# Moving the self-loop term of a graph layer into the adjacency chunk on the Pool, and the expert counts with it

## The chip, the cores and the metric

One core of a Trainium2 chip. Five engines work side by side and meet through semaphores: TensorE (PE), VectorE (DVE), ScalarE (ACT), GpSimd (the Pool) and SyncE (SP), which here only issues DMAs. The metric is the time of one execution in microseconds, less is better.

## The reference

```
def layer(x, adj, kernel, bias, beta, Wr, br, W1, b1, W2, b2):
    z = layernorm(x)                                  # x: 4096 x 128
    scale = 1 / (sum(adj, axis=1) + beta)
    agg = adj @ z + beta[:, None] * z                 # adj: 4096 x 4096, float32
    x = x + scale[:, None] * agg @ kernel + bias
    z = layernorm(x)
    logits = z @ Wr + br                              # 64 experts
    top2, idx = top_k(logits, 2);  gates = softmax(top2)
    return x + sum over the 2 experts e of a row: gate_e * (relu(z @ W1[e] + b1[e]) @ W2[e] + b2[e])
```

## The kernel before

The 4096 rows are cut into 32 tiles of 128. Eight groups g of four tiles (512 columns of the transposed adjacency) are worked one after the other. The adjacency of a group comes in eight chunks k of 1 MB, each holding four tiles of source rows by the group's 512 columns, by DMAs that SP issues (`load_chunk`, L373) into a ring of five buffers, `adj_sb`. A buffer is loaded again when its chunk has been read: after the DVE's `low_part` for a split chunk, after the PE's products for a whole one.

Group 0 and chunk 7 of each later group are whole: the PE multiplies float32 chunks as they are (L883). Chunks 0 to 6 of groups 1 to 7 are split: ACT rounds the chunk (`round_chunk`, L550) into one of three `high` buffers, the DVE subtracts (`low_part`, L668) into `low`, and the PE makes three products of them (L893, L894, L897). `high` of a chunk may be written when the chunk three before has been used. ACT has these chunks in one row, with the other work of the previous group between them: the copy of the sum (`copy_agg`, L554) ahead of chunk 3, the root ahead of chunk 4, `normalise` (L565) ahead of chunk 5 and `copy_z1t` (L571) ahead of chunk 6.

The term beta * z is a product of its own: the Pool copies the group's z tiles to `zi` (L474), makes `diag`, four 128 x 128 blocks identity times beta (L475), and the PE multiplies them into the same bank at the end of the group (`own_product`, L876).

The previous group is finished while the PE multiplies the present one, at fixed steps of its chunks. `gnn` (L849) stands in chunk 0, `turn_z1` (L855) at the start of chunk 4, `router` (L861) at the start of chunk 5 and `ranks` (L866 to L869) in the middle of chunk 6. The DVE does `residual`, `shifts`, and after chunk 6's `low_part` the choice of two experts (`choose`, L694 to L708), which ends with `mask`. `ranks` waits for `mask`. Then come `low_part` of the next group's chunk 0 and `place` (L712 to L719), which makes the counts `more` and `seen` and the rows' targets, `slot`.

The Pool's `dispatch(g)` copies the normalised rows to `payload` (L481, L482), waits once for `prefilled` (eight padding DMAs of the rows' DRAM tensor, which SP issues among the chunks of groups 1 and 2, L396) and for `slot`, issues eight indirect DMAs (L488, "scatters") and waits until all have landed, since all share one semaphore; `normalise(g)` waits for the landed scatters of group g - 2. `own_rows(g + 2)` stands ahead of `dispatch(g)` on the Pool.

After the eighth group a list of expert tiles is made, and the expert part runs (L950 to L966 on the PE, L507 on the Pool), then the output. The change touches none of that.

## Time and profile before

| | us |
|---|---|
| median of 3 runs | 421.05 (419.92 to 421.44) |
| the profiled execution | 419.54, of which the span of the trace is 417.7 |
| group 0 | up to 41 |
| groups 1 to 7 | 41 to 236 |
| tail of group 7 and the list | 236 to 270 |
| expert part | 270 to 393 |
| output | 393 to 418 |

Busy shares of the whole span are PE 85%, DVE 72%, POOL 56%, ACT 39%; they average stages with different limits. The group stage is read on its own: from one group's end to the next, which wait ends last, and whether it is so in every group. The time between two ends is about 27.3 us in groups 4 to 6, and 28 to 28.6 us in groups 1, 2, 3 and 7.

### The profile page before, as it was taken

What the parts mean: (1) busy time and instruction counts of PE and PEld (TensorE: products, weight loads), DVE (VectorE), ACT (ScalarE), POOL (GpSimd) and SP (SyncE); (2) the same over time, 40 slices, a digit from 0 to 9 for tenths busy, and PEclk for the clock granted to TensorE, in tenths of its full rate; (3) what the DMA queues carried; (4) which work ended last, traced back from release to release, by engine and by line L of the source; (5) the groups of instructions that cost most, each with busy time, mean ns of one, the idle gap of its engine ahead of it and who ended that gap; (6) DMA issues with size and microseconds to landing.
All of it is one profiled execution on the core that took longest, in us unless ns stands there. A gap on an engine that the chain in (4) does not pass through costs nothing.

```text
span 417.7 us, 8267 instructions
## 1 busy us (share of the span) xinstructions
PE 353.5 (85%) x2029; PEld 283.0 (68%) x2029; DVE 299.8 (72%) x881; ACT 163.7 (39%) x260; POOL 233.2 (56%) x219
## 2 busy tenths in 40 slices
PE   5999999979989999999998727199999999999300
PEld 2445777867858768778686423199999999999200
DVE  4644989779798997988987347066777777777157
ACT  3445654754845738548454030011212111112153
POOL 3450003076583885858838654246777777777600
PEclk9799999999999999999999958689999999999855
DMA  8999998997968969879691110779999999996087
GB/s 295 367 424 362 395 424 313 420 427 286 398 239 357 359 230 421 326 264 374 236 399 42 40 40 30 211 215 290 300 306 303 310 292 289 300 291 215 27 335 269
DMA packets 45479, 119.25 MB, mean 286 GB/s; under 512 B 7689, under 2 KB 19614, under 8 KB 37266
## 3 DMA queue, kind: packets, MB, share of 16 engines
q1 hardware_dynamic: 27794, 95.88, 61.9%
q10 hardware_dynamic: 12672, 14.58, 11.7%
q0 software_dynamic: 4992, 8.54, 5.7%
q8 instruction: 9, 0.15, 0.1%
q14 instruction: 12, 0.10, 0.1%
HBM read 104.02 MB, written 16.78 MB: 289 GB/s over the span
## 4 chain that ended last, share of the span: by engine, by line
PE 35%; POOL 22%; DMA 18%; issue 11%; DVE 10%; ACT 3%; POOLq 1%; SPq 0%; ACTq 0%; DVEq 0%
POOL dispatched_rows L488 16%; DMA dispatched_rows<-payload,slot 10%; PE bank L956 8%; PE bank L883 7%; PE bank L966 4%; PE bank_pair L966 4%; DMA expert_answers<-adj_ring,ans 3%; DVE adj_low L668 3%; PE bank L950 2%; POOL diag L475 2%; PE bank_pair L963 2%; PE bank L963 2%; DVE x_sb L824 2%; POOL payload L481 2%; DMA adj_ring<-adj_t 2%
## 5 line engine op out<-in xcount | busy, mean ns | idle before, releaser
L668 DVE TENSOR_TENSOR adj_low<-adj_ring,adj_high 128x2048 fp32r<-128x2048 f32 x49 | 113.8, 2332 | 27.7 <-ACT adj_high L550 27.6
L550 ACT CAST adj_high<-adj_ring 128x2048 fp32r<-128x2048 f32 x49 | 93.3, 1907 | 67.4 <-PE bank L897 40.5
L488 POOL DMA_INDIRECT dispatched_rows<-payload,slot x64 | 95.3, 1489 | 36.9 <-issue 29.0
L507 POOL DMA_INDIRECT expert_answers<-adj_ring,ans x92 | 90.5, 983 | 41.0 <-ACT adj_ring L600 20.9
L893 PE MATMUL bank<-adj_high,z_hi 128*128 128x512 f32 x196 | 79.6, 406 | 0.0
L894 PE MATMUL bank<-adj_high,z_lo 128*128 128x512 f32 x196 | 76.6, 391 | 0.0
L803 DVE TENSOR_SCALAR adj_ring<-bank,adj_ring 128x128 f32<-128x128 f32 x184 | 56.0, 346 | 14.4 <-PE bank L956 11.9
L883 PE MATMUL bank<-adj_ring,z_sb 128*128 128x512 f32 x120 | 55.9, 619 | 3.2 <-DVE z_sb L654 3.2
L956 PE MATMUL bank<-xt_sb,adj_ring 128*128 128x128 f32 x368 | 57.1, 278 | 0.0
L897 PE MATMUL bank<-adj_low,z_hi 128*128 128x512 f32 x196 | 52.7, 390 | 0.0
L956 PEld LDWEIGHTS bank<-xt_sb,adj_ring 128*128 128x128 f32 x368 | 49.5, 195 | 0.0
L474 POOL COPY zi<-z_sb 128x512 f32<-128x512 f32 x8 | 8.5, 1063 | 66.0 <-PE bank L876 37.5
L883 PEld LDWEIGHTS bank<-adj_ring,z_sb 128*128 128x128 f32 x120 | 23.7, 199 | 30.5 <-issue 29.4
L897 PEld LDWEIGHTS bank<-adj_low,z_hi 128*128 128x128 f32 x196 | 36.8, 188 | 8.1
L600 ACT COPY adj_ring<-bank_pair 128x128 f32<-128x128 f32 x46 | 11.3, 267 | 77.9 <-PE bank_pair L966 76.5
L894 PEld LDWEIGHTS bank<-adj_high,z_lo 128*128 128x128 f32 x196 | 36.9, 188 | 6.6
L893 PEld LDWEIGHTS bank<-adj_high,z_hi 128*128 128x128 f32 x196 | 36.9, 188 | 6.5
L950 PE MATMUL bank<-ident,adj_ring 128*128 128x128 f32 x92 | 26.3, 286 | 9.3 <-DMA adj_ring<-dispatched_rows 9.0
L793 DVE COPY xt_sb<-bank 128x128 f32<-128x128 f32 x92 | 25.7, 280 | 10.9 <-PE bank L950 10.9
L966 PE MATMUL bank_pair<-adj_ring 128*128 128x128 f32 x184 | 28.8, 280 | 0.4 <-DVE adj_ring L803 0.3
L966 PE MATMUL bank<-adj_ring 128*128 128x128 f32 x184 | 28.5, 277 | 0.2 <-DVE adj_ring L803 0.2
L798 DVE TENSOR_TENSOR ans<-adj_ring,skip_tab 128x1 int32<-128x1 f32 x92 | 14.7, 160 | 18.5 <-DMA expert_answers<-adj_ring,ans 15.6
(129 smaller groups left out, 430.5 us busy)
## 6 DMA issues: line engine op xcount, KB each, us to landing
adj_ring<-adj_t SPq DMA_DIRECT2D x64, 1024.0 KB, 8.9
adj_ring<-w_pack SPq DMA_DIRECT2D x48, 257.5 KB
adj_ring<-w_pack ACTq DMA_DIRECT2D x44, 257.5 KB
dispatched_rows<-pad_rows SPq DMA_DIRECT2D x8, 528.0 KB, 10.9
adj_ring<-expert_answers SPq DMA_DIRECT2D x8, 512.0 KB, 7.0
adj_ring<-dispatched_rows SPq DMA_DIRECT2D x48, 66.0 KB
adj_ring<-dispatched_rows ACTq DMA_DIRECT2D x44, 66.0 KB
out<-x_sb SPq DMA_DIRECT2D x8, 256.0 KB, 4.3
```

Source lines behind the costliest of these rows:

```text
L488: pool.indirect_dma_start(rows, bass.IndirectOffsetOnAxis(ap=slot[:, b, i:i + 1], axis=0), payload[:, b, t, k, :], None).then_inc(scattere ...
L507: pool.indirect_dma_start(y_tok, bass.IndirectOffsetOnAxis(ap=ans[:, s:s + 1], axis=0), y_sb[:, s, :], None, bounds_check=N * K - 1, oob_i ...
L550: nc.scalar.copy(high[:, m % PARTS], adj_sb[:, slot_of(g, k)]).then_inc(hi_ready, 1)
L668: v.tensor_tensor(low[:, m % PARTS], adj_sb[:, slot_of(g, k)], high[:, m % PARTS].bitcast(F32), ALU.subtract).then_inc(lo_ready, 1)
L803: last = v.tensor_scalar(h_sb[:, s % DEEP, c, :], up_ps[s % 2][:, c * P:(c + 1) * P], w_sb[:, s, B1_COL + c:B1_COL + c + 1], 0.0, ALU.add, ...
L883: last = mm(agg_ps[g % 2][:], z_sb[:, k * CJ + u, :], adj_sb[:, slot_of(g, k), u, :], start=(k + u == 0), stop=False)
L893: mm(agg_ps[g % 2][:], z_hi[:, j, :], high[:, m % PARTS, u, :], start=(j == 0), stop=False)
L894: mm(agg_ps[g % 2][:], z_lo[:, j, :], high[:, m % PARTS, u, :], start=False, stop=False)
L897: last = mm(agg_ps[g % 2][:], z_hi[:, k * CJ + u, :], low[:, m % PARTS, u, :], start=False, stop=False)
L950: nc.tensor.transpose(xt_ps[s % 2][:, 0:P], xin[:, s, 0:D], ident[:]).then_inc(x_turned, 1)
L956: last = mm(up_ps[s % 2][:, c * P:(c + 1) * P], w_sb[:, s, c * P:(c + 1) * P], xt_sb[:, s % 2, :], start=True, stop=True)
L966: last = mm(y, h_sb[:, s % DEEP, c, :], w_sb[:, s, H + c * D:H + (c + 1) * D], start=False, stop=(c == HC - 1))
```

## The change

Beta * z no longer has a product. Since adj @ z + beta * z is (adj + diag(beta)) @ z, the Pool adds `diag` to the four diagonal blocks of the chunk that holds them, in the ring, by two additions: three blocks of 128 columns, then the last one. `own_product` and `zi` are gone. The chunk with the diagonal (chunk g of group g) is loaded seventh in groups 0 to 6; in group 7 it is chunk 7, the eighth, and whole. The z tiles are made in that order, in six batches in place of five. ACT's rounding of the chunk (the PE's product in groups 0 and 7) waits for `diag_added`.

`add_diag` stands on the Pool: groups 0 and 1 ahead of `dispatch(0)`; group 2 in `dispatch(0)` ahead of its scatters; groups 3 to 6 between the fourth and the fifth scatter of `dispatch(1)` to `dispatch(4)`; group 7 after the scatters of `dispatch(5)`. `more` and `seen` go from the DVE to the Pool, ahead of the scatters. `choose` of the next group waits for `seen` before it writes `mask`. The cast `chosen` and the eight small `diff` subtractions are gone (one `diff` at the end). The scatters of the two payload buffers have a semaphore each; the Pool no longer waits for them to land, `normalise` waits for its own buffer's.

```diff
-BATCHES = ((0, 4), (4, 4), (8, 8), (16, 8), (24, 8))
-X_BEFORE = (1, 3, 4, 5)
+BATCHES = ((4, 4), (8, 4), (12, 8), (20, 8), (0, 4), (28, 4))
+X_BEFORE = (1, 3, 4, 6)
+DIAG_AT = [CHUNKS - 2] * (GROUPS - 1) + [CHUNKS - 1]
...
+def chunk_order(g):
+    if g == GROUPS - 1:
+        return list(range(CHUNKS))
+    others = [k for k in range(CHUNKS - 1) if k != g]
+    return others + [g, CHUNKS - 1]
...
+            def add_diag(g):
+                k = DIAG_AT[g]
+                own.after(pool.tensor_tensor(diag[:], ident[:, None, :].to_broadcast([P, GT, P]),
+                                             beta_sb[:, group(g)].to_broadcast([P, GT, P]), ALU.mult))
+                pool.wait_ge(adj_in[slot_of(g, k)], landed(g, k))
+                chunk = adj_sb[:, slot_of(g, k)].rearrange("p u n -> p (u n)")
+                most = (CJ - 1) * (GN + P)
+                blocks = chunk[:, 0:most].rearrange("p (u n) -> p u n", u=CJ - 1)[:, :, 0:P]
+                pool.tensor_tensor(blocks, blocks, diag[:, 0:CJ - 1, :], ALU.add)
+                own.after(pool.tensor_tensor(chunk[:, most:most + P], chunk[:, most:most + P], diag[:, CJ - 1, :], ALU.add))
+                pool.sem_inc(diag_added, 1)
...
             def dispatch(g):
                 b = g % 2
                 pool.wait_ge(z1_ready, g + 1)
                 pool.tensor_copy(payload[:, b, :, 1, 0:D], payload[:, b, :, 0, 0:D])
                 own.after(pool.tensor_copy(payload[:, b, :, :, ANSWER], answer_tab[:, group(g), :]))
-                pool.wait_ge(prefilled, 16 * PAD_DMAS)
+                pool.wait_ge(mask_ready, g + 1)
+                own.after(pool.tensor_tensor(more[:], mask[:, 0:2, :], mask[:, 2:4, :], ALU.add))
+                own.after(pool.tensor_tensor(more[:, 0, :], more[:, 0, :], more[:, 1, :], ALU.add))
+                pool.wait_ge(rank_done, g + 1)
+                pool.tensor_tensor(seen[:], seen[:], more[:, 0, :], ALU.add).then_inc(seen_ready, 1)
+                if g == 0:
+                    add_diag(2)
+                    pool.wait_ge(prefilled, 16 * PAD_DMAS)
                 pool.wait_ge(slots_ready, g + 1)
                 for t in range(GT):
+                    if t == 2 and 0 < g < GROUPS - 3:
+                        add_diag(g + 2)
                     for k in range(K):
...
-                pool.wait_ge(scattered, (g + 1) * (GT * K * 16))
-                pool.sem_inc(payload_free, 1)
...
+                if g == GROUPS - 3:
+                    add_diag(GROUPS - 1)
...
                 act.wait_ge(adj_in[slot_of(g, k)], landed(g, k))
+                if k == DIAG_AT[g]:
+                    act.wait_ge(diag_added, g + 1)
...
             def copy_agg(g):
-                act.wait_ge(agg_done, g + 1)
+                act.wait_ge(chunk_used, (g + 1) * CHUNKS)
...
                 if g >= 2:
-                    act.wait_ge(payload_free, g - 1)
+                    act.wait_ge(scattered[g % 2], all_scattered(g - 2))
...
-                own.after(v.tensor_copy(chosen[:], top_i[:, :, 0:K]))
...
+                if g > 0:
+                    dve.wait_ge(seen_ready, g)
                 v.tensor_tensor(mask[:], hot[:, :, 0, :], hot[:, :, 1, :], ALU.add).then_inc(mask_ready, 1)
 
             def place(g):
-                dve.wait_ge(mask_ready, g + 1)
-                own.after(v.tensor_reduce(more[:], mask[:].rearrange("p t e -> p e t"), AX_X, ALU.add))
                 dve.wait_ge(rank_done, g + 1)
-                v.tensor_tensor(seen[:], seen[:], more[:], ALU.add).then_inc(seen_ready, 1)
...
-                for t in range(GT):
-                    last = mm(agg_ps[g % 2][:, t * P:(t + 1) * P], zi[:, t, :], diag[:, t, :], start=False, stop=(t == GT - 1))
-                last.then_inc(agg_done, 1)
```

On the Pool, in the program's order from one group's `dispatch` to the next (`waits` names the semaphores that an instruction waits for), the kernel before:

```order
L488 DMA dispatched_rows<-payload,slot 262144x132 x7
L474 COPY zi<-z_sb 128x512 [waits scattered,agg_done]
L475 TENSOR_TENSOR diag<-ident,beta_sb 128x512
L481 COPY payload<-payload 128x4x128 [waits z1_ready]
L482 COPY payload<-answer_tab 128x8
L488 DMA dispatched_rows<-payload,slot 262144x132 [waits slots_ready,prefilled,pool_own]
L488 DMA dispatched_rows<-payload,slot 262144x132 x7
```

and the changed one, `dispatch(1)`:

```order
L514 COPY payload<-payload 128x4x128 [waits z1_ready]
L515 COPY payload<-answer_tab 128x8
L517 TENSOR_TENSOR more<-mask 128x128 [waits mask_ready,pool_own]
L518 TENSOR_TENSOR more<-more 128x64 [waits pool_own]
L520 TENSOR_TENSOR seen<-seen,more 128x64 [waits rank_done,pool_own]
L529 DMA dispatched_rows<-payload,slot 262144x132 [waits slots_ready]
L529 DMA dispatched_rows<-payload,slot 262144x132 x3
L495 TENSOR_TENSOR diag<-ident,beta_sb 128x512
L501 TENSOR_TENSOR adj_ring<-adj_ring,diag 128x3x128 [waits adj_in0,pool_own]
L502 TENSOR_TENSOR adj_ring<-adj_ring,diag 128x128
L529 DMA dispatched_rows<-payload,slot 262144x132 [waits pool_own]
L529 DMA dispatched_rows<-payload,slot 262144x132 x3
```

The wait for landed scatters is gone, the counts have come in ahead of the scatters, and the diagonal with its wait for a landed chunk stands among them.

On ACT, from the copy of group 0's sum to chunk 6 of group 1, before:

```order
L554 COPY agg_sb<-bank 128x512 [waits agg_done]
L550 CAST adj_high<-adj_ring 128x2048 [waits chunk_used,adj_in1]
L558 ACTIVATE std<-mv,eps_sb 128x4 [waits var1]
L550 CAST adj_high<-adj_ring 128x2048 [waits chunk_used,adj_in2]
L565 ACTIVATE payload<-x_sb,shift,rstd 128x128 [waits shift_ready]
L565 ACTIVATE payload<-x_sb,shift,rstd 128x128 x3
L550 CAST adj_high<-adj_ring 128x2048 [waits chunk_used,adj_in3]
L571 COPY z1t<-bank 128x512 [waits z1_turned]
L550 CAST adj_high<-adj_ring 128x2048 [waits chunk_used,adj_in4]
```

and changed:

```order
L594 COPY agg_sb<-bank 128x512 [waits chunk_used]
L590 CAST adj_high<-adj_ring 128x2048 [waits chunk_used,adj_in1]
L598 ACTIVATE std<-mv,eps_sb 128x4 [waits var1]
L590 CAST adj_high<-adj_ring 128x2048 [waits chunk_used,adj_in2]
L605 ACTIVATE payload<-x_sb,shift,rstd 128x128 [waits shift_ready]
L605 ACTIVATE payload<-x_sb,shift,rstd 128x128 x3
L590 CAST adj_high<-adj_ring 128x2048 [waits chunk_used,adj_in3]
L611 COPY z1t<-bank 128x512 [waits z1_turned]
L590 CAST adj_high<-adj_ring 128x2048 [waits chunk_used,diag_added,adj_in4]
```

The order is the same; the copy of the sum hangs on the last chunk, and the seventh rounding on the Pool's additions too.

On the DVE, from `mask` to the targets, before:

```order
L708 TENSOR_TENSOR mask<-hot 128x256 [waits dve_own]
L668 TENSOR_TENSOR adj_low<-adj_ring,adj_high 128x2048 [waits hi_ready]
L712 TENSOR_REDUCE more<-mask 128x64 [waits mask_ready]
L714 TENSOR_TENSOR seen<-seen,more 128x64 [waits rank_done,dve_own]
L716 TENSOR_TENSOR work<-hot,bank 128x4x64 x2
```

and changed, in the second group on:

```order
L746 TENSOR_TENSOR mask<-hot 128x256 [waits seen_ready,dve_own]
L709 TENSOR_TENSOR adj_low<-adj_ring,adj_high 128x2048 [waits hi_ready]
L751 TENSOR_TENSOR work<-hot,bank 128x4x64 [waits rank_done]
L751 TENSOR_TENSOR work<-hot,bank 128x4x64
```

Two counts have left the DVE, and `mask` waits for the Pool's count of the group before.

## Rows read from the trace of the kernel before

**Rows 1.** Engines' busy time in one stretch, group 5:

```profile
core 0: us, PE busy (x) PEld busy (x) DVE busy (x) ACT busy (x) POOL busy (x), PEclk, DMA share, GB/s
153.50:180.90 27.40, 26.49 (x127) 20.57 (x126) 24.28 (x46) 16.16 (x14) 19.86 (x13) 1.00 0.84 327
```

**Rows 2.** Who waited for whom: us in total, times, longest:

```profile
POOL zi L474 <- DMA dispatched_rows<-payload,slot: 28.5, 5, 6.8
PEld bank L866 <- DVE mask L708: 15.6, 8, 3.7
```

**Rows 3.** Timeline of PE: first ranks product in groups 2 and 5 (start us, us, ...):

```profile
90.92 0.28 PE L866 MATMUL bank<-mask,before 128*128 128x256 bf16 x1 [2.13 <-DVE mask L708]
174.08 0.28 PE L866 MATMUL bank<-mask,before 128*128 128x256 bf16 x1 [0.91 <-DVE mask L708]
```

**Rows 4.** Timeline of ACT: the rounding of chunk 6 in groups 1, 2, 3, 5, 7:

```profile
54.64 1.91 ACT L550 CAST adj_high<-adj_ring 128x2048 fp32r<-128x2048 f32 x1
83.17 1.91 ACT L550 CAST adj_high<-adj_ring 128x2048 fp32r<-128x2048 f32 x1 [1.10 <-DMA adj_ring<-adj_t]
111.73 3.71 ACT L550 CAST adj_high<-adj_ring 128x2048 fp32r<-128x2048 f32 x2
166.36 1.91 ACT L550 CAST adj_high<-adj_ring 128x2048 fp32r<-128x2048 f32 x1
221.88 1.91 ACT L550 CAST adj_high<-adj_ring 128x2048 fp32r<-128x2048 f32 x1
```

**Rows 5.** Timeline of PE: own products that end groups 1, 2, 4 and 6:

```profile
68.05 1.05 PE L876 MATMUL bank<-diag,zi 128*128 128x128 f32 x8
96.67 1.05 PE L876 MATMUL bank<-diag,zi 128*128 128x128 f32 x8
152.45 1.05 PE L876 MATMUL bank<-diag,zi 128*128 128x128 f32 x8
207.15 1.05 PE L876 MATMUL bank<-diag,zi 128*128 128x128 f32 x8
```

**Rows 6.** Chunk 6's load in groups 1 (last of two), 2, 6: issue and landing:

```profile
L373 SPq DMA_DIRECT2D adj_ring<-adj_t x2: 593/642/691, 41.3 to 41.9; - x2
DMA to landing us min/median/max: 10.3/11.2/12.2
...
L373 SPq DMA_DIRECT2D adj_ring<-adj_t x1: 1184/1184/1184, 70.8 to 70.8; - x1
DMA to landing us min/median/max: 12.4/12.4/12.4
...
L373 SPq DMA_DIRECT2D adj_ring<-adj_t x1: 432/432/432, 180.9 to 180.9; - x1
DMA to landing us min/median/max: 10.8/10.8/10.8
```

**Rows 7.** Timeline of DVE and POOL where they meet, groups 1, 4 and 5:

```profile
53.64 2.29 DVE L668 TENSOR_TENSOR adj_low<-adj_ring,adj_high 128x2048 fp32r<-128x2048 f32 x1 [1.07 <-ACT adj_high L550]
134.68 3.20 DVE L668 TENSOR_TENSOR adj_low<-adj_ring,adj_high 128x2048 fp32r<-128x2048 f32 x1
134.69 1.03 POOL L475 TENSOR_TENSOR diag<-ident,beta_sb 128x512 f32<-128x512 f32 x1
135.68 2.67 POOL L481 COPY payload<-payload 128x512 f32<-128x512 f32 x1
165.71 2.29 DVE L668 TENSOR_TENSOR adj_low<-adj_ring,adj_high 128x2048 fp32r<-128x2048 f32 x1 [1.32 <-ACT adj_high L550]
```

**Rows 8.** Timeline of POOL: a two-input operation, group 0's first scatter, its last:

```profile
10.68 1.26 POOL L464 TENSOR_TENSOR z_lo<-z_sb,z_hi 128x512 fp32r<-128x512 f32 x1 [5.80 <-ACT z_hi L534]
85.42 3.02 POOL L488 DMA_INDIRECT dispatched_rows<-payload,slot  x1 [11.96 <-issue]
101.54 0.96 POOL L488 DMA_INDIRECT dispatched_rows<-payload,slot  x1 [0.30 <-issue]
```

**Rows 9.** Timeline of DVE: the cast that the change drops, group 3:

```profile
117.96 0.16 DVE L704 CAST chosen<-top_i 128x8 f32<-128x8 uint32 x1
```

More of the change, by code:

```diff
@@ L59, in batch_of, with half_made @@
 def batch_of(j):
-    return max(b for b, (first, _) in enumerate(BATCHES) if first <= j)
+    return next(b for b, (first, count) in enumerate(BATCHES) if first <= j < first + count)
+def half_made(b):
+    return sum(count // 2 for _, count in BATCHES[:b])
 def dve_half(b):
@@ L408, in _ @@
                 load_weights(sp, starts[s], s)
-            sp.wait_ge(scattered, 16 * TILES * K)
+            for b in range(2):
+                sp.wait_ge(scattered[b], all_scattered(GROUPS - 2 + b))
             for s in range(SP_SLOTS):
@@ L743, in _ @@
             place(GROUPS - 1)
+            v.tensor_tensor(diff[:], top[:, :, 1], top[:, :, 0], ALU.subtract).then_inc(diff_ready, 1)
             dve.wait_ge(total_done, 1)
```

123 lines of the change are left out of this document (59 added, 64 removed).

## The prediction

> **What bounds the kernel now.** I read first the busy times of one group, then who waited for whom, then the timelines of PE, ACT, DVE and Pool at one place of every group. In a group of 27.4 us the PE is busy for 26.5 [rows 1], so each of its products looks like time. But the waits say that in every group it stands still before `ranks`, for the DVE's `mask` [rows 2], and two timelines show that this wait sets the pace. Chunk 6 is rounded from 83.17 in group 2 and `ranks` starts at 90.92, 7.75 us later; in group 5 from 166.36 to 174.08, 7.72 us [rows 3, 4]. Between lie the rounding (1.91 us), `low_part` (2.29), and `choose`. From `ranks` to the own product it is 5.75 us (90.92 to 96.67) [rows 3, 5]. So a group ends some 13.4 us after ACT starts on its chunk 6, and what counts is when that rounding starts. I call the start of the last group's own product T. In group 5, T is 152.45 and the rounding starts 13.9 us later; in group 2 it is 68.05 and 15.1; in group 3 96.67 and 15.1; in group 7 207.15 and 14.7 [rows 4, 5].
>
> The other clock is the load of chunk 6. It stands in SP's row behind that of chunk 4, which needs the buffer of the last group's chunk 7, so it is issued just after T. In group 2 it is issued at 70.8 and lands 12.4 us later, at 83.2, and ACT starts then and there: no slack. In group 1 it lands at 41.9 + 12.2 = 54.1, against a start at 54.64: slack 0.5. In group 6 at 180.9 + 10.8 = 191.7 [rows 4, 6], and with T one group of 27.4 us after 152.45 that is 11.9 us after T; slack is 1 to 2.5 us in the calm groups. The change puts Pool work into exactly this gap, behind the landing and ahead of the rounding.
>
> **What is removed.** An own product of 1.05 us [rows 5] leaves each group; its critical part is about 0.95. Group 0 gives nothing: ACT is busy with the chunk it rounds from 40.0 and copies the sum after that, so `gnn` starts at the same time. In groups 1 and 2 the start of the rounding hangs on a landing, which does not come earlier with it. `chosen`, a cast of 0.16 us [rows 9], and `diff` leave `choose`: `mask` comes 0.25 us earlier in each group. `more` and `seen` leave `place`, which is not on the way to `mask`; the next `low_part`s come earlier, which the copy of the sum does not wait for. The Pool's waits for landed scatters (28.5 us in five [rows 2]) go, and with them the late `normalise` of groups 3 and 7.
>
> **What is added, on the path.** The two additions on the Pool have two full inputs. The nearest row is a subtraction of 512 columns in 1.26 us [rows 8]; by columns 384 and 128 of them take 0.95 and 0.35, and with signals some 1.45 us. That is the lower bound. The upper bound comes from the meeting with the DVE. At 134.68 `low_part` is issued while the Pool makes `diag` until 135.72; it takes 3.20 in place of 2.29 us. The Pool's next copy, issued at 135.68, ends at 138.35, after `low_part`, and takes 2.67 us [rows 7]. So either engine waits for the other's whole instruction, and a waiting `low_part` goes in between two Pool instructions. Meeting one costs the additions up to 2.3 us more.
>
> The Trainium skill, "SBUF — State Buffer", section "SBUF: two separate sides", says the same of two inputs, and that who starts first has the shared pair for one whole instruction. But in its section "Who interferes with whom" it takes a `tensor_tensor` of the DVE to leave descriptor generation alone (inferred there). Here scatters beside `low_part` take up to 3.02 us and others 0.96 [rows 8]. By that page the eight scatters would take 8 x 1.26 = 10.1 us and the term of group 3 below would be 0; the sum would be 2.2 us less. The rows decide.
>
> *Group 1.* Chunk 6 lands at 54.1, while `low_part` runs from 53.64 to 55.93 [rows 6, 7]. The additions run behind it, to about 57.2; the rounding starts at 57.3 in place of 54.64: +2.65, less 0.25, is +2.4. Bare it would be +0.7.
>
> *Group 2.* T is 2.4 later; the loads were busy around it, so the landing moves by about 2 us, to 85.2. `low_part` of chunk 5, which also waits for its load, ends at about 85.6; the additions end at 87.0, the rounding starts at 87.1, 3.9 late in all. Less 0.25 this is 3.6, so +1.2 more.
>
> *Group 3.* The first scatter of `dispatch(0)` stood until 85.42 for the padding rows [rows 8]; they too come 2.2 later. Eight scatters took from 85.42 to 102.50, 17.1 us (first and last of eight in [rows 8]). From 87.6 they end at 104.7. The copies and the counts (five short instructions with waits, 2.0 us by their sizes) end at 106.7, four scatters (half of 17.1) at 115.2, `diag` and the additions with signals at 117.8. T has moved to 100.3, so the rounding starts 17.5 after T in place of 15.1: +2.4, less 0.25, is +2.2. Were the Pool in time, it would be -1.9; with two more meetings, +4.
>
> *Groups 4 to 6.* Here the Pool has caught up: scatters start about 1.5 us before T, four take some 7.5 us, and it stands ready before the landing at 11.5 to 12.0 after T. What is on the PE is 0.95 earlier, so `low_part` of chunk 5, at 165.71 in group 5 [rows 7], would come 12.3 after T; `diag` on the Pool meets `low_part` of chunk 3 and may push it to 12.9. The first addition runs until 12.5 to 12.9, so the second arrives just when `low_part` does. If it slips in first, the rounding starts at 13.35 in place of 13.9: -0.55 and -0.25, -0.8 a group. If not, the second addition ends at about 15.1 and the rounding starts at 15.5: +1.6 and -0.25, +1.35. The rows don't tell which; I take half of each, +0.3 a group, +0.8 for three.
>
> *Group 7 and the tail.* Its diagonal is in chunk 7, landed and added long before it is read. The rounding of chunk 6 starts 13.0 after T in place of 14.7: -2.0 with `choose`. The last own product is on the path: -0.95. `chosen`, `diff` and `seen` before the last targets: -0.35. The Pool's last count runs beside the DVE's `work`. The expert part is unchanged.
>
> **The sum.** 2.4 + 1.2 + 2.2 + 0.8 - 2.0 - 0.95 - 0.35 = +3.3 us. The profiled execution took 419.54, so 422.9. It lies 1.5 under the median of the runs, 421.05; set on the median, 424.4 us, 0.8% slower. About 0.5% (2.1 us) is what a measurement of this kernel can tell from no change.
>
> **The rivals.**
> 1. *The additions always slip in* in groups 4 to 6: -2.4 in place of +0.8, so 421.2 us. For it speaks that `diag` on the Pool delays the DVE by itself; against it that the landing in group 6 is 11.9 after T, which leaves 0.1.
> 2. *They always meet* `low_part`: 3 x 1.35 = 4.05 in place of 0.8, 427.6 us, and 429.5 with group 3 at +4. For it speaks that four scatters will load the DMA engines just while chunk 6 comes.
> 3. *The other side, faster:* the Pool's instructions come through nearly bare, because the waits of a Pool instruction fall between `low_part`s more often than in these rows. Then group 1 is +0.7, group 2 +0.9, group 3 (Pool in time) -1.9, groups 4 to 6 -2.4, the rest -3.3: -6.0, 415.0 us. It decides at the additions: under about 1.5 us from landing to `diag_added` the kernel is faster, over 2.5 us slower. Against it: the Pool's first scatter hangs on the padding in any case, and in group 1 `low_part` runs at the landing.
>
> **How the numbers follow.** The forecast has 0.47 (422 to 427.5; 0.09 of it within 0.5%), rival 1 0.20 (0.14 within, 0.03 on either side), rival 2 0.15, rival 3 0.18. Faster by over 0.5%: 0.18 + 0.03 = 0.21. Within: 0.09 + 0.14 = 0.23. Slower: 0.38 + 0.03 + 0.15 = 0.56. The range goes from rival 3's 415 to 430, the end of rival 2 with a late group 3; beyond are additions of still other length.
>
> **What would show it.** In the changed kernel's trace: the additions in 1.3 us alone and up to 3.6 beside `low_part`; ACT's idle time before chunk 6 put down to the Pool; `ranks` still waiting for `mask`, 7.4 us after the rounding starts; ends of groups 1 and 2 at about 70.4 and 100.3; the rounding of group 3 behind the Pool's additions, at about 118. What would make it wrong: `ranks` waiting for something else, or a landing of chunk 6 that moves against T by a microsecond, which turns groups 4 to 6 all one way.

## The result, and the profile after

The changed kernel takes 431.89 us (median of 4 runs, 428.82 to 432.39), the kernel before 420.49 beside it (416.96 to 421.44). The ratio is 1.0272 with a 95% interval of 1.0194 to 1.0349: slower, and by more than three times the 0.8% that was forecast. The forecast was 424.4 with a range of 415 to 430. The profiled execution took 432.21 us (span 430.4, mean granted clock 0.917), against 419.54, 417.7 and 0.935 of before.

Who waited for whom in the changed kernel (us in total, times, longest). L501 is the first addition, L904 the first product of `ranks`, L746 `mask`:

```profile
POOL adj_ring L501 <- DMA adj_ring<-adj_t: 50.8, 5, 22.1
PEld bank L904 <- DVE mask L746: 24.2, 8, 4.6
PE bank L904 <- DVE mask L746: 21.1, 8, 4.2
```

The wait for landed scatters of [rows 2] is gone. The wait of the PE's weight load for `mask` has grown from 15.6 us to 24.2. The place of the loss is the group stage. I measure each group from one start of ACT's copy of the sum to the next, since both kernels have it. Before: 27.3, 28.6, 28.5, 27.3, 27.4, 27.3, 28.1 us for groups 1 to 7. After, each in one row (the columns as in [rows 1]):

```profile
42.50:70.20 27.70, 26.34 (x114) 20.34 (x115) 23.02 (x41) 16.14 (x15) 8.15 (x8) 0.94 0.94 372
70.20:102.50 32.30, 28.09 (x119) 21.17 (x118) 25.19 (x43) 16.17 (x14) 14.15 (x10) 0.89 0.83 326
102.50:133.70 31.20, 27.22 (x119) 20.91 (x118) 23.75 (x42) 15.96 (x14) 27.66 (x23) 0.95 0.73 289
133.70:164.20 30.50, 27.09 (x119) 20.73 (x118) 24.51 (x42) 16.05 (x14) 22.27 (x17) 0.94 0.75 293
164.20:190.90 26.70, 25.57 (x119) 19.67 (x118) 23.10 (x41) 16.16 (x14) 18.87 (x16) 1.00 0.87 335
190.90:221.40 30.50, 27.20 (x119) 20.51 (x118) 27.18 (x43) 15.99 (x14) 25.36 (x18) 0.94 0.74 294
221.40:248.30 26.90, 25.65 (x118) 19.43 (x116) 18.42 (x39) 10.38 (x11) 23.50 (x19) 1.00 0.47 182
```

Two things stand in these rows. Group 5 takes 26.7 us and its neighbours 30.5, with nearly the same instructions in them. And the two are told apart by the granted clock: 1.00 in groups 5 and 7, under it in all others.

**The two fates of the second addition.** Timelines of the Pool and the DVE in groups 4 and 5 (start, duration):

```profile
145.84 1.02 POOL L501 TENSOR_TENSOR adj_ring<-adj_ring,diag 128x384 f32<-128x384 f32 x1 [5.17 <-DMA adj_ring<-adj_t]
146.63 2.38 DVE L709 TENSOR_TENSOR adj_low<-adj_ring,adj_high 128x2048 fp32r<-128x2048 f32 x1 [1.32 <-ACT adj_high L590]
146.81 2.50 POOL L502 TENSOR_TENSOR adj_ring<-adj_ring,diag 128x128 f32<-128x128 f32 x1
```

```profile
176.16 1.01 POOL L501 TENSOR_TENSOR adj_ring<-adj_ring,diag 128x384 f32<-128x384 f32 x1 [4.92 <-DMA adj_ring<-adj_t]
177.13 0.46 POOL L502 TENSOR_TENSOR adj_ring<-adj_ring,diag 128x128 f32<-128x128 f32 x1
177.21 4.75 DVE L709 TENSOR_TENSOR adj_low<-adj_ring,adj_high 128x2048 fp32r<-128x2048 f32 x2 [1.32 <-ACT adj_high L590]
```

In group 4 `low_part` was issued at 146.63, inside the first addition, and came in between the two: the second took 2.50 us. In group 5 the second addition began 0.08 us ahead of `low_part` and took 0.46. Group 6 went like group 4 (203.97, 2.50).

**What followed on the PE.** Its first product of `ranks` in groups 2, 4 and 5 (the wait before it in brackets):

```profile
94.33 0.39 PE L904 MATMUL bank<-mask,before 128*128 128x256 bf16 x1 [4.21 <-DVE mask L746]
156.81 0.28 PE L904 MATMUL bank<-mask,before 128*128 128x256 bf16 x1 [3.41 <-DVE mask L746]
185.09 0.28 PE L904 MATMUL bank<-mask,before 128*128 128x256 bf16 x1 [1.12 <-DVE mask L746]
```

and the stretches behind these three products, the clock in the third column from the right:

```profile
94.00:96.00 2.00, 1.67 (x7) 1.42 (x8) 2.00 (x2) 1.87 (x1) 1.70 (x2) 0.50 1.01 423
96.00:98.00 2.00, 2.00 (x6) 1.54 (x5) 1.93 (x6) 0.00 (x0) 1.70 (x2) 0.50 0.63 245
98.00:100.00 2.00, 2.00 (x5) 1.13 (x5) 2.00 (x2) 1.07 (x1) 1.69 (x2) 0.67 0.15 50
```

```profile
156.80:159.00 2.20, 2.19 (x10) 1.79 (x11) 2.20 (x1) 0.00 (x0) 2.20 (x2) 0.62 0.82 338
159.00:161.00 2.00, 2.00 (x6) 1.50 (x5) 1.93 (x6) 0.07 (x1) 1.76 (x5) 0.56 0.00 0
161.00:164.00 3.00, 3.00 (x9) 1.33 (x7) 3.00 (x2) 1.82 (x1) 2.84 (x2) 1.00 0.00 0
```

```profile
185.00:187.00 2.00, 1.91 (x12) 1.65 (x13) 2.00 (x2) 0.41 (x1) 2.00 (x2) 1.00 0.81 312
```

After its wait of 4.21 us the PE ran at 0.50, which is 1.2 GHz, until about 99.2, some 5 us. After 3.41 us the stretches at 0.62 and 0.56 hold both levels; cut into half microseconds they show 0.50 from 157.5 to 160.5. After 1.12 us it ran at 1.00, 2.4 GHz. From `ranks` to the copy of the sum it is 5.93 us in group 5, and 8.28, 7.53, 7.52 and 7.59 in groups 2, 3, 4 and 6. With the removed product in them these stretches were 6.84 us before, in every group.

So the chain has one link more than the prediction has: the additions make the rounding late, the rounding `mask`, `mask` lengthens the wait of the PE, and behind the long wait much of the rest of the group runs at half speed. Theory A, then: the clock lengthens the ends of groups 2, 3, 4 and 6 by 2.33 + 1.58 + 1.57 + 1.64 = 7.1 us.

Not all of that reaches the end of the kernel. The seventh rounding of group 3 waits for the Pool:

```profile
118.87 1.91 ACT L590 CAST adj_high<-adj_ring 128x2048 fp32r<-128x2048 f32 x1 [3.31 <-POOLq L503]
```

and the Pool works from 87.87 (the first scatter of `dispatch(0)`) to 118.74 with no gap over 0.31 us. It had no slack for an earlier end of group 2 to use, so the 2.33 us of group 2 were covered by it. An estimate of what the clock cost is therefore 1.58 + 1.57 + 1.64 = 4.8 us. Rival B: the loads and the Pool set the end of each group in any case, and the clock only fills a gap.

### The profile page after: what moved, and what is told of

Its sections match the earlier page's. It is cut to its first block, busy times and chain, and to the rows that moved or that the text cites. A ratio compares the mean times of both kernels' runs of the same rounds, so it can differ in the third digit from the quotient of the medians.

```text
span 430.4 us, 8171 instructions
## 1 busy us (share of the span) xinstructions
PE 354.3 (82%) x1965; PEld 281.7 (65%) x1965; DVE 302.9 (70%) x852; ACT 163.8 (38%) x261; POOL 261.7 (61%) x251
## 4 chain that ended last, share of the span: by engine, by line
PE 43%; DVE 20%; DMA 16%; POOL 9%; ACT 5%; issue 5%; POOLq 1%; SPq 1%; DVEq 0%; ACTq 0%
DMA adj_ring<-adj_t 10%; DVE adj_low L709 9%; PE bank L989 9%; PE bank L918 8%; POOL dispatched_rows L529 5%; PE bank_pair L999 5%; PE bank L999 4%; ACT adj_high L590 4%; PE bank L932 3%; DMA expert_answers<-adj_ring,ans 3%; PE bank L983 2%; PE bank L928 2%; PE bank L929 2%; PE bank_pair L996 2%; PE bank L996 2%
## 5 line engine op out<-in xcount | busy, mean ns | idle before, releaser
L709 DVE TENSOR_TENSOR adj_low<-adj_ring,adj_high 128x2048 fp32r<-128x2048 f32 x49 | 119.0, 2441 | 38.2 <-ACT adj_high L590 38.1
L529 POOL DMA_INDIRECT dispatched_rows<-payload,slot x64 | 96.7, 1511 | 22.6 <-issue 17.5
L928 PE MATMUL bank<-adj_high,z_hi 128*128 128x512 f32 x196 | 83.9, 428 | 0.0
L929 PE MATMUL bank<-adj_high,z_lo 128*128 128x512 f32 x196 | 78.5, 401 | 0.0
L932 PE MATMUL bank<-adj_low,z_hi 128*128 128x512 f32 x196 | 56.7, 414 | 0.0
L932 PEld LDWEIGHTS bank<-adj_low,z_hi 128*128 128x128 f32 x196 | 39.5, 202 | 9.0
L918 PEld LDWEIGHTS bank<-adj_ring,z_sb 128*128 128x128 f32 x120 | 24.2, 204 | 32.1 <-issue 29.0
L928 PEld LDWEIGHTS bank<-adj_high,z_hi 128*128 128x128 f32 x196 | 37.9, 193 | 8.8 <-issue 1.7
L929 PEld LDWEIGHTS bank<-adj_high,z_lo 128*128 128x128 f32 x196 | 38.0, 194 | 8.5 <-issue 1.7
L501 POOL TENSOR_TENSOR adj_ring<-adj_ring,diag 128x384 f32<-128x384 f32 x8 | 11.0, 1372 | 51.0 <-DMA adj_ring<-adj_t 50.8
```

Of the source, the lines that this page charges most:

```text
L529: pool.indirect_dma_start(rows, bass.IndirectOffsetOnAxis(ap=slot[:, b, t, k:k + 1], axis=0), payload[:, b, t, k, :], None).then_inc(scatt ...
L709: v.tensor_tensor(low[:, m % PARTS], adj_sb[:, slot_of(g, k)], high[:, m % PARTS].bitcast(F32), ALU.subtract).then_inc(lo_ready, 1)
L918: last = mm(agg_ps[g % 2][:], z_sb[:, j, :], adj_sb[:, slot_of(g, k), u, :], start=(k + u == 0), stop=(k + 1 == CHUNKS and u + 1 == CJ))
L928: mm(agg_ps[g % 2][:], z_hi[:, first + u, :], high[:, m % PARTS, u, :], start=(k + u == 0), stop=False)
L929: mm(agg_ps[g % 2][:], z_lo[:, first + u, :], high[:, m % PARTS, u, :], start=False, stop=False)
L932: last = mm(agg_ps[g % 2][:], z_hi[:, first + u, :], low[:, m % PARTS, u, :], start=False, stop=False)
```

## The experiments

### Without the additions, and with their work but not their waits

In the first the additions and the waits for them are gone. In the second the Pool makes additions of the same size in a tile of its own, which nobody waits for. Both leave the term beta * z out of the result.

```diff
x_noadd, x_scratch:
                 if k == DIAG_AT[g]:
-                    act.wait_ge(diag_added, g + 1)
x_scratch:
+                pool.tensor_tensor(scratch[:, 0:CJ - 1, :], z_sb[:, 0:CJ - 1, :], diag[:, 0:CJ - 1, :], ALU.add)
+                own.after(pool.tensor_tensor(scratch[:, CJ - 1, :], z_sb[:, CJ - 1, :], diag[:, CJ - 1, :], ALU.add))
```

> The changed kernel without the additions to the diagonal and without the waits for them; the self-loop term beta * z is left out. Counts on the Pool, the order of chunks and the two semaphores stay. Theory A (the additions stand between landing and rounding in groups 2 to 4 and 6, and the half clock follows from that wait): groups 3 to 6 take 26.2 to 26.7 us each as group 5 did with the additions, the clock falls only in group 1, the time is 414 to 418 us, ratio 0.985 to 0.995. Rival C (the counts and the scatters that run late on the Pool slow the DVE through the place where both meet): groups stay at 28 us or more, ratio 1.005 or more.

> The changed kernel in which the Pool makes the same two additions at the same places and with the same wait for the landed chunk, but of z tiles into a tile of their own, and neither ACT nor PE waits for them; beta * z is left out. Theory A (the wait is the cost, not the Pool's work): within 2 us of the kernel without additions, 414 to 420 us, ratio 0.985 to 0.998. Rival C (the additions cost by holding off the DVE's subtraction): 422 us or more, ratio 1.005 or more.

Measured: 414.25 us without them, 0.9832 of before (0.978 to 0.9885); 417.69 with the idle work, 0.992 (0.9889 to 0.9951). So the additions cost 17.6 us of the 431.89: some 3.4 for the Pool's work itself, and 14.2 because others wait for it. Without them groups 4 to 7 take 26.2 to 26.5 us each. That is the 1.1 us under before which the removed product promised, and it was there to be had. With the idle work the PE stood 2.16 us before `ranks` in group 3 and 2.37 in group 7, the clock fell to 0.50 behind both, and they took 29.4 and 29.5 us.

### Is it the clock? The PE kept busy with filling products

The PE gets products that nobody reads ahead of the two places where it stands still: before the first product of `gnn` of group 0 (8 of them) and before `ranks` (a number for each group, in the second version larger).

```diff
+                if g == 0:
+                    warm(8, spare_bank)
                 pe.wait_ge(agg_copied, g + 1)
...
             def ranks(g):
+                warm((0, 12, 12, 8, 4, 8, 4, 0)[g], spare_bank)    # x_fill
+                warm((10, 12, 12, 10, 10, 10, 4, 0)[g], spare_bank) # x_fill2
                 pe.wait_ge(mask_ready, g + 1)
```

> The changed kernel with products of ones put on the PE where it stood longest: 8 before it waits for the copy of group 0's sum, and 12, 12, 8, 4, 8, 4 before the wait for mask in groups 2 to 7. They go to a bank that nobody reads then. Each takes about 0.22 us at the full clock. Theory A (the PE's clock is granted at half for some microseconds behind a stall of 3 us or more, which cost 1.3 us in group 1 and 2.4, 1.7, 1.7 and 1.7 in groups 2, 3, 4 and 6): the stalls become shorter than 2.2 us, the granted clock stays at 1.0 from group 1 to 7, and 6 to 8.5 us of the added time go away: 423 to 426 us, ratio 1.005 to 1.013. Rival B (the half clock is a sign of the waiting and costs nothing, the PE would wait for the DVE or for a load in those microseconds anyway): the time stays at 430 to 433, ratio 1.025 or more.

Measured: 433.82 us (1.0272, 1.0207 to 1.0336). No gain in the whole, which by the number alone speaks for rival B. The filling was too thin in two places: in group 1 a wait of 3.05 us was left and the stretch from `ranks` to the copy took 8.80 us, in group 5 2.42 us and 7.53. In groups 2, 3, 4 and 6, where 1.5 to 1.6 us were left, it took 5.93 to 5.96. And in group 5 the second addition was blocked (2.50 us). So the second version fills groups 1 and 5 as well.

> The changed kernel with filling products as in the first such kernel, and more of them where a stall was left: 8 ahead of the copy of group 0's sum, and 10, 12, 12, 10, 10, 10, 4 ahead of mask in groups 1 to 7. In the first one the clock fell where a stall of 2.4 or 3.1 us was left (groups 5 and 1: 7.5 and 8.8 us from ranks to the end of the group) and not where it was 1.6 us or less (5.9 us). Theory A: with all stalls under 1.8 us the half clock is gone from groups 1 to 6, each of them has 5.8 to 6.0 us from ranks to its end, groups take 28.5 to 29 us where the second addition waits for a subtraction of the DVE: 427 to 430 us, ratio 1.015 to 1.022. Rival B (the half clock costs nothing in the end): 432 to 434 us, ratio 1.027 or more.

Measured: 428.44 us (1.0179, 1.0098 to 1.026), as theory A expected, and 3.4 us under the changed kernel, though the intervals of the two ratios overlap. Three of its seven groups:

```profile
42.30:70.60 28.30, 27.02 (x124) 20.15 (x125) 23.50 (x41) 16.23 (x15) 8.18 (x8) 1.00 0.94 369
70.60:100.90 30.30, 28.53 (x131) 20.68 (x130) 23.45 (x43) 16.17 (x14) 12.21 (x9) 1.00 0.87 345
...
159.90:188.80 28.90, 27.78 (x129) 20.57 (x128) 25.58 (x42) 15.99 (x15) 24.88 (x17) 1.00 0.81 309
```

The clock is at 1.00 in all seven. Groups 4, 5 and 6 all take 28.9 us with the second addition blocked in each. That is 1.5 us over before, where the prediction had priced the blocked case at 1.35; groups 2 and 3 take 30.3 and 30.1 (its steps give 29.9 and 30.6). With the clock kept up, then, its steps hold for groups 2 to 6 within about half a microsecond. Group 7 does not fit them: 28.0 us against 28.1 before, where 2.0 less was forecast. The time is near that of the prediction's second rival, in which every addition of groups 4 to 6 is blocked (427.6).

In the profiled executions the group stage ends 2.8 us earlier than in the changed kernel (245.60 against 248.39). Group 3 ends 2.8 earlier (from `ranks` to the copy it was 1.6 faster, and its additions, unblocked this time, were done 1.2 earlier), groups 4 and 6 give 1.7 each, group 5 loses 2.2 with its free passage, group 7 loses 1.1. Behind the group stage it gains another 1.8 us, which the fillers don't explain: the expert part and the output, from the first copy to `xt_sb` on the DVE to the end, took 146.8 us here and 149.2 in the changed kernel, and over the profiled executions of all sixteen kernels, none of which changes that part, it varies from 146.7 to 149.2. So the clock is shown where the rows show it, in the ends of the groups, and less sharply in the total.

### Does a longer path to the rounding come out as it stands? One copy more

The Pool makes a copy of 1024 columns between the additions and their signal in groups 3 to 6.

```diff
+                if 2 < g < GROUPS - 1:
+                    own.after(pool.tensor_copy(scratch[:], z_sb[:, 0:8, :]))
                 pool.sem_inc(diag_added, 1)
```

> The changed kernel with one more Pool instruction, a copy of 1024 columns (some 1.2 us by the 0.62 us of a copy of 512), between the additions and their signal in groups 3 to 6. If the path from the landing over the Pool's additions to the rounding sets each group's end, each of the four groups gets 1.2 us longer, and group 5, whose stall of 1.1 us grows over 2.3, falls to the lower clock and gets another 1.5: 6 to 7.5 us in all, 437.5 to 439.5. Against the other reading, in which the loads set the pace and the Pool only fills their slack, under 2 us come: 431.5 to 434.

Measured: 441.13 us (1.0508, 1.0452 to 1.0565), 9.2 over the changed kernel by the medians, more than the 6 to 7.5 expected, and 7.3 by the profiled executions (439.52 against 432.21). The copy and `ranks` in groups 4 and 5:

```profile
151.69 1.04 POOL L505 COPY scratch<-z_sb 128x1024 f32<-128x1024 f32 x1
160.21 0.28 PE L907 MATMUL bank<-mask,before 128*128 128x256 bf16 x1 [4.21 <-DVE mask L749]
181.09 2.98 POOL L505 COPY scratch<-z_sb 128x1024 f32<-128x1024 f32 x1
191.56 0.39 PE L907 MATMUL bank<-mask,before 128*128 128x256 bf16 x1 [4.18 <-DVE mask L749]
```

Group 3 gets 2.2 us longer, group 6 0.4. Group 4, whose clock fell already, gets 0.8 us longer by a copy of 1.04. Group 5 gets 4.6 longer: the copy met `low_part` and took 2.98, and the wait before `ranks`, 4.18 in place of 1.12, now cost the clock. It did so with its additions still unblocked (1.01 and 0.46 at 179.59). Rival B, by which under 2 us would come, is out; that every group pays the same is not borne out either.

### Group 1: the right number for the wrong reason

The prediction had group 1 late by 2.4 us because its additions meet `low_part`. It was late as forecast, but the additions took 1.19 and 0.45 us, unblocked (at 54.62 and 55.77). What was late was the start, on the PE:

```profile
43.30 1.13 PE L885 MATMUL bank_pair<-gnn_w_and_degree,agg_sb 128*128 128x129 f32 x8 [2.89 <-ACT agg_sb L594]
45.17 0.63 PE L929 MATMUL bank<-adj_high,z_lo 128*128 128x512 f32 x1
48.38 0.40 PE L929 MATMUL bank<-adj_high,z_lo 128*128 128x512 f32 x1
```

The first product of `gnn` waits for ACT's copy of the sum, which stands on ACT behind a rounding that waits for its load (from 40.78). The PE stood 2.89 us there, where it stood 0.48 before, and then its products took 0.63 in place of 0.40 us until 48. Of the longer wait the missing own product is only about 1.0 us. The load came 0.8 us later (that rounding started at 40.00 before), and group 0's other products were done about 1.0 earlier. That the load matters as much shows in `x_sems` (below), which keeps the own product:

```profile
43.71 1.13 PE L848 MATMUL bank_pair<-gnn_w_and_degree,agg_sb 128*128 128x129 f32 x8 [2.15 <-ACT agg_sb L552]
46.00:48.00 2.00, 2.00 (x6) 1.51 (x6) 1.91 (x11) 0.00 (x0) 0.00 (x0) 0.50 0.95 393
```

There the rounding before the copy started at 41.18, the clock fell, and chunk 6 of group 1 was rounded from 57.38, as late as in the changed kernel (57.00) and with no addition at all. The test puts ACT's copy ahead of that rounding (chunk 2 of group 1) in the changed kernel:

```diff
-            for k in range(PARTS):
+            for k in range(PARTS - 1):
                 round_chunk(1, k)
+            copy_agg(0)
+            round_chunk(1, PARTS - 1)
             for g in range(1, GROUPS):
-                copy_agg(g - 1)
+                if g > 1:
+                    copy_agg(g - 1)
```

> The changed kernel with one thing moved: ACT copies group 0's sum ahead of the rounding of chunk 2 of group 1, not behind it. It tells apart two causes for the 2.4 us by which group 1 ended late. Theory A (the PE stood 2.89 us before the first product of the graph layer's tail, because that copy stood behind a rounding, and then ran at half clock): the stall falls under 1.5 us, the rounding of chunk 3 of group 1 no longer starts 2 us late, the copy of group 1's sum starts at 68.0 to 68.7 in place of 70.3, the whole takes 429 to 430.5 us. Rival B (the Pool's additions in the seventh chunk hold group 1): the stall goes, but the copy still starts at 70 or later, and the whole stays at 431.5 to 432.5.

Measured: 433.51 us (1.0332, 1.028 to 1.0384), against the changed kernel's 1.0272 (1.0194 to 1.0349): no gain, so nearer rival B's number, though 1 us above it, with the stall gone as A wants. Why, in group 1:

```profile
53.62 2.29 DVE L712 TENSOR_TENSOR adj_low<-adj_ring,adj_high 128x2048 fp32r<-128x2048 f32 x1 [1.31 <-ACT adj_high L590]
53.69 3.09 POOL L501 TENSOR_TENSOR adj_ring<-adj_ring,diag 128x384 f32<-128x384 f32 x1 [20.83 <-DMA adj_ring<-adj_t]
57.33 1.91 ACT L590 CAST adj_high<-adj_ring 128x2048 fp32r<-128x2048 f32 x1 [3.27 <-issue]
64.69 0.39 PE L907 MATMUL bank<-mask,before 128*128 128x256 bf16 x1 [4.21 <-DVE mask L749]
64.70:67.00 2.30, 2.30 (x9) 1.88 (x10) 2.30 (x2) 0.00 (x0) 2.22 (x1) 0.50 0.99 397
```

The group starts on time, so `low_part` runs from 53.62 when the chunk lands, the addition waits behind it, and the rounding starts at 57.33. That is the prediction's step for group 1 ("at 57.3"). But the PE had been early, stood 4.21 us and fell to half clock, and the copy of the sum came at 72.96, against 70.32 in the changed kernel. Of these 2.6 us, 2.3 are the clock: from `ranks` to the copy it is 8.27 us in place of 5.95, and `ranks` itself came only 0.3 later (64.69 against 64.37). The early stall had hidden the other mechanism: it made `low_part` late (55.99), and so let the additions through.

### The semaphores alone

The kernel before, with a semaphore for each payload buffer; the Pool doesn't wait for its scatters.

> The kernel before with one part of the change: a semaphore for each payload buffer's scatters, and the Pool not waiting for them to land. Theory A: the Pool has 5 to 7 us less in each group, the late normalise of groups 3 and 7 starts 1.4 to 1.7 us earlier, nothing else was waiting for the Pool: 417.5 to 419.5 us, ratio 0.993 to 0.997. Rival E (the Pool, now ahead, meets the DVE in other places and costs there what it gives): no difference, ratio 0.998 to 1.003.

Measured: 419.93 us, 0.9985 (0.9945 to 1.0024), no difference that can be told. In the profiled execution groups 2 to 6 are as before, and group 7 takes 27.3 in place of 28.1 us. Group 1 takes 28.9 in place of 27.3, by the late load and the stall shown above. The 28.5 us of waiting in [rows 2] had hidden little; a gain of some 0.8 us in group 7 is all that the rows show, and the total can't confirm it.

### The counts alone

The changed kernel with `more` and `seen` made by the DVE, in `place`, and the choice not waiting for them.

```diff
-                own.after(pool.tensor_tensor(more[:], mask[:, 0:2, :], mask[:, 2:4, :], ALU.add))
-                own.after(pool.tensor_tensor(more[:, 0, :], more[:, 0, :], more[:, 1, :], ALU.add))
...
-                pool.tensor_tensor(seen[:], seen[:], more[:, 0, :], ALU.add).then_inc(seen_ready, 1)
...
             def place(g):
...
+                own.after(v.tensor_reduce(more[:], mask[:].rearrange("p t e -> p e t"), AX_X, ALU.add))
                 dve.wait_ge(rank_done, g + 1)
+                v.tensor_tensor(seen[:], seen[:], more[:], ALU.add).then_inc(seen_ready, 1)
```

> The changed kernel with one part undone: the counts (more, seen) are made by the DVE again, and the choice of the experts no longer waits for them. They cost the Pool 0.4 + 0.3 + 0.3 us, or 3.0 where one of them meets a subtraction, and the DVE 0.60 + 0.23 in the kernel before. If the changed kernel loses by its additions alone, this one takes as long, within 2 us of 431.9: only group 3, where the Pool is late, may start its additions 1 to 2.5 us earlier, and the DVE pays 0.8 us behind the mask, where nothing waits. Rival: the counts hold the Pool, so that the additions of groups 3 to 6 come late too; then 425 to 428 us.

Measured: 435.67 us (1.0387, 1.033 to 1.0443), 3.8 over the changed kernel's median, though the intervals overlap, and outside what either reading expected. The move of the counts is thus no cause of the loss; it may have been worth a few us. In group 5, where the additions went free in the changed kernel:

```profile
175.00 1.02 POOL L501 TENSOR_TENSOR adj_ring<-adj_ring,diag 128x384 f32<-128x384 f32 x1 [2.89 <-DMA adj_ring<-adj_t]
175.96 2.51 POOL L502 TENSOR_TENSOR adj_ring<-adj_ring,diag 128x128 f32<-128x128 f32 x1
```

the second addition is now blocked, the wait before `ranks` 3.24 us and the group 30.4. The DVE's timing has moved, and with it who meets whom. A like pair is below (`x_last3` and `x_last4`), where the counts on the DVE cost 3.3 us, 415.19 against 418.47, and there the intervals of the ratios don't overlap.

### The additions elsewhere

First the chunk with the diagonal eighth and whole in every group, added behind all eight scatters. The whole chunk then needs all 32 tiles of z in two parts.

```diff
-DIAG_AT = [CHUNKS - 2] * (GROUPS - 1) + [CHUNKS - 1]
+DIAG_AT = [CHUNKS - 1] * GROUPS
...
-                    if t == 2 and 0 < g < GROUPS - 3:
-                        add_diag(g + 2)
...
+                if 0 < g < GROUPS - 2:
+                    add_diag(g + 2)
```

> The changed kernel with the chunk of the diagonal loaded last in every group, as group 7 has it: it is whole, the PE alone reads it, some 8 us after it lands. Chunk 7 is split in its place, so z's high and low parts have four tiles more. The Pool adds after all eight scatters. Everything is computed. Theory A: no wait between landing and rounding is left; groups 3 to 6 take about 26.5 us, the clock falls in group 1 only: 414 to 418 us, ratio 0.985 to 0.995, faster than both kernels. Rival D (the Pool with eight scatters ahead is late and the PE waits at the last chunk): groups of 28 us or more, ratio above 1.01.

Measured: 432.15 us (1.0244, 1.0192 to 1.0295). Groups 5 and 6 take 26.2 and 26.8 us, but in group 3 the Pool is late by its first scatters, and the PE waits for it:

```profile
134.16 5.89 PE L913 MATMUL bank<-adj_ring,z_sb 128*128 128x512 f32 x8 [8.51 <-POOLq L500]
```

That group took 38.2 us. The next version only moves the additions forward among the scatters (behind the 4th in `dispatch(1)`, the 6th in the next four, in place of behind all eight).

```diff
                 for t in range(GT):
+                    if 0 < g < GROUPS - 2 and t == (2 if g == 1 else 3):
+                        add_diag(g + 2)
```

> The kernel with the diagonal's chunk last in every group, with the additions moved forward on the Pool: behind the fourth scatter of dispatch(1) (group 3's) and behind the sixth of dispatch(2) to dispatch(5), in place of behind all eight. In the one with all eight ahead group 3 took 38.2 us, since the PE waited 8.5 us for the Pool at the last chunk and then had half the clock, and group 7 took 29.5, since its additions met choose. Groups 4 to 6 took 26.2 to 29.1. Theory A: group 3 about 28 and group 7 about 27 us, so 417 to 422 us, ratio 0.992 to 1.003. Rival D (the Pool has too little time in any order): 426 us or more.

Measured: 417.95 us (0.9945, 0.9897 to 0.9992); groups 5 to 7 take 26.8 us each. With ACT's copy of group 0's sum moved as above (`x_last3`), and with the counts on the DVE besides (`x_last4`):

> The kernel with the additions in the eighth chunk, placed among the scatters (4th of the second dispatch, 6th of the next four), and with the copy of group 0's sum ahead of the rounding of chunk 2. If the stall at the start of group 1 costs that kernel (417.95) what it costs the changed one, 1 to 2 us go: 415.5 to 417.5 us. Rival: group 1 there was already at 68.19, as early as the loads allow, and nothing comes: 417.5 to 418.5.

> The kernel of 415.19 us (additions in the eighth chunk, copy of group 0's sum first) with the counts on the DVE again. By the same reasoning there is nothing to win: 414.5 to 417 us. Rival: 0.8 us of the DVE in every group stand in the way of the next group's first subtractions and of the last targets: 418 to 421.

Measured: 415.19 us (0.9884, 0.9835 to 0.9932) and 418.47 (0.9973, 0.9943 to 1.0003). `x_last3` computes all that the kernel before does and is 1.2% faster. Its waits before `ranks` are 1.24 to 1.55 us in all groups but the fourth (2.37), and the clock stays at 1.00 from 146 to 154, behind that one, too. In `x_last4` group 3 takes 30.3 us in place of 28.9: its first addition (114.60) takes 2.95 us, where it was 1.01 in `x_last3`.

Second, the diagonal and its additions on the DVE, ahead of the subtraction that would meet them:

```diff
                 low_part(g, 4)
+                if g != 2 and g < GROUPS - 1:
+                    add_diag(g)                 # on the DVE
                 low_part(g, 5)
+                if g == 2:
+                    add_diag(g)
                 low_part(g, 6)
                 choose(g - 1)
+                if g == GROUPS - 1:
+                    add_diag(g)
```

> The changed kernel with diag and the additions on the DVE, between its subtractions: ahead of that of chunk 5 (behind it in group 2; in group 7 behind choose). Everything else as changed. The DVE has some 3 us to spare in a group; the three instructions take about 1.3 us (0.6, 0.4, 0.2) and meet nothing of their own engine. Theory A: no addition waits for a subtraction, the rounding of chunk 6 starts 12.5 to 13.5 us after the group's start, no stall above 2 us: 415 to 419 us, ratio 0.987 to 0.997. Rival F (the wait for the landing now holds the DVE and its whole row): groups of 28 us, 425 us or more.

> The kernel with the diagonal and its additions on the DVE, and the copy of group 0's sum ahead of the rounding of chunk 2. There group 1 ended at 70.81 and group 2 took 31.9 us with a stall of 4.2 us. Theory A: group 1 ends at 68 to 69, group 2 follows its load, 1.5 to 2.5 us earlier: 413.5 to 415.5 us against 416.4. Rival: group 2 ends where it did, because something other than the load of its seventh chunk holds it: 416 to 417.

Measured: 416.36 us (0.9877, 0.9801 to 0.9952), and with the moved copy of the sum 418.18 (0.9946, 0.992 to 0.9972), which is a miss. On the DVE the additions take 0.56 and 0.28 us and nothing blocks them; groups 3 to 7 take 26.1 to 26.4. Groups 1 and 2 spoil it: 27.9 and 31.9, and with the moved copy 30.6 and 33.1, since the PE, early again, stands 3.16 and 4.20 us before `ranks`:

```profile
63.14 0.39 PE L920 MATMUL bank<-mask,before 128*128 128x256 bf16 x1 [3.16 <-DVE mask L754]
95.30 0.39 PE L920 MATMUL bank<-mask,before 128*128 128x256 bf16 x1 [4.20 <-DVE mask L754]
```

So with the moved copy the median fell where the additions are off the path to `ranks` (`x_last3`) and rose where they lie on it (`x_swap`, `x_dve3`), by 1.6 to 2.8 us each; the intervals overlap in each pair.

## Why the prediction was wrong

The direction, the place and the chain were right; the size was off by 7.5 us, and the time fell outside the range. The profiled execution (432.21) is 9.3 us over the prediction's sum of 422.9. By its own steps:

- **The path through the rounding of chunk 6** (the bound): right. In group 2 the rounding starts at 86.97 (forecast 87.1), `ranks` comes 7.36 us after it (7.4), groups 1 and 2's roundings and the end of group 1, 70.3 (70.4), stand where they were put.
- **From `ranks` to the end of the group, 5.75 us in every case**: this is the step that failed, and the largest part of the error. The prediction worked out how late the rounding would be, and took the rest as fixed. But what makes `ranks` late makes the PE wait, and the longer wait was followed by the lower clock. To the copy of the sum, which starts 0.2 us later still, it was 7.5 to 8.3 us in four groups, and 5.93 to 5.95 where the clock held. The blocked case was priced at +1.35 us for groups 4 to 6; it cost 3.2 in groups 4 and 6 (30.6 and 30.5 against 27.3), and 1.5 where the fillers kept the clock up (`x_fill2`). Of the 9.3 us some 4.8 are this, those of groups 3, 4 and 6; group 2's 2.3 were covered, as shown above. The rest, estimated from the same rows: 1.1 by the end of group 3, 1.7 since two of the three groups 4 to 6 were blocked in place of half, 0.7 in group 7, and 1.6 in the expert part, which the change does not touch. The tail gave 0.6 more than forecast. The 1.6 are within what that part varies by in the profiled executions (146.7 to 149.2 us in sixteen kernels, 147.5 before, 149.2 in the changed kernel).
- **Group 1, +2.4**: right number, wrong reason, and so luck, as `x_swap` shows. The sentence that group 0 gives nothing, because "`gnn` starts at the same time", left out that the PE stands idle until then, and what the stall brings with it. Part of that stall is a load that came later in this execution.
- **Group 2, +1.2**: the group is 3.7 us longer than before, 2.3 of them the clock, so 1.3 without it.
- **Group 3, +2.2**: its rounding starts at 118.87 (about 118), behind the Pool; `diag` and additions were late as worked out, with the first addition blocked (2.94 us). Its group is 2.7 us longer than before, 1.6 of them the clock. The 1.1 left are less than 2.2 because group 2 had ended late already, while the Pool's row stayed where it was.
- **Groups 4 to 6, half of each case**: one went free (26.7 us, 0.7 under before; forecast -0.8) and two were blocked. The two bounds were met, the weight lay on the upper.
- **Group 7, -2.0**: -1.3. The tail, from the end of group 7 to the first product of the expert part, came out at about -1.9 against -1.3.
- **The Pool's landed-scatter waits**: worth nothing that can be measured (`x_sems`), as the sum had it but for group 7.

The range ended at 430 for the same reason. Its upper end was rival 2 with a late group 3, that is all terms at their dearest, with a PE whose products always take the same time. Without the 4.8 us of the clock the median would be about 427 us, inside the range (an estimate from the rows above).

What is not settled is when the clock falls. In the 14 kernels other than `before` and `x_sems` I can read the wait before `ranks` against the stretch behind it, 98 groups. Behind 17 waits of 3.30 to 4.21 us the granted clock fell every time (the stretch took 7.3 to 8.7 in place of 5.95 us). Behind the 63 of up to 1.70 us no stretch was long for the clock (three are long for other reasons: late additions or loads ahead of the eighth chunk). Of the 18 between, 1.92 to 3.27 us, eleven were followed by a fall, and seven were not, two of them behind 3.25 and 3.27 us. The first of these:

```profile
91.07 0.28 PE L899 MATMUL bank<-mask,before 128*128 128x256 bf16 x1 [3.25 <-DVE mask L741]
91.00:93.00 2.00, 1.93 (x12) 1.65 (x13) 1.11 (x2) 1.42 (x2) 1.54 (x2) 1.00 0.99 418
```

(from `x_last2`, group 2: the wait, and the clock at 1.00 behind it), while behind 2.16 us in `x_scratch` the clock was at 0.50. What decides between these I have not found. The Trainium skill ("TensorE: Matmul & The Clock Gate", "Part 1: The HAM clock gate") states that this gate has two levels and none between. The trace agrees: cut into half microseconds the rows above show 0.50 and 1.00, and other values (0.68 at 99.00, 0.74 at 160.50) only where one passes into the other.

## What to carry to other kernels

Where the PE waits once in every group, a delay on the path to that wait is not paid once: price the wait that it makes, and then the stretch behind the wait at both levels of the clock (in the changed kernel +1.6 to +2.3 us on 5.95). Before adding such losses up, ask of each group whether another engine holds the next one anyway, as the Pool held group 3. Removing work from an engine that waits just behind it makes that wait longer, so ask what it had kept busy. And an instruction of the Pool that shares the path with long two-input instructions of the DVE should be put where they don't run, or on the DVE itself, ahead of them: whether it slips in was decided by 0.1 to 0.2 us in groups 4 and 5, and edits elsewhere moved it (`x_fill`, `x_counts`, `x_swap`).

## What the runs showed of the hardware

- Two additions in a row on the Pool are not one unit: a waiting DVE instruction came in between them (146.63, above), so the short second one (0.45 us bare) took 2.50 us, more than the first.
- The scatters, which the Pool issues, are held up by two-input subtractions as well: 2.87 us at 132.90 in the changed kernel, while the DVE made two of them (130.30 to 134.89), and 0.97 for the three after it. The Trainium skill ("SBUF — State Buffer", "Who interferes with whom") infers that such an operation leaves them alone; the rows, as in [rows 8], say otherwise.
- A stall can protect. With the stall at the start of group 1 the additions slipped in; without it they were blocked and the group ended 2.6 us later, 2.3 of them by the clock.
- The same two additions took 1.4 us bare and 3.4 to 3.6 blocked on the Pool, and 0.8 on the DVE.
